# Narrow cross attention: four PSUM banks for scores, one pair for maxima, three key buffers, maxima three steps ahead

## What is computed

```python
def _L1_xattn_ref(queries, keys, values, valid_lens, Wq, Wk, Wv, Wo):
    ...
    q = split_heads(queries @ Wq)
    k = split_heads(keys @ Wk)
    v = split_heads(values @ Wv)
    scores = jnp.einsum('bhqd,bhkd->bhqk', q, k) / jnp.sqrt(jnp.float32(hd))
    mask = jnp.arange(skv)[None, None, None, :] < valid_lens[:, None, None, None]
    scores = jnp.where(mask, scores, NEG)
    p_attn = jax.nn.softmax(scores, axis=-1)
    out = jnp.einsum('bhqk,bhkd->bhqd', p_attn, v)
    out = out.transpose(0, 2, 1, 3).reshape(b, sq, D)
    return out @ Wo
```

## Time and profile before

| what | value |
|---|---|
| median of 3 runs | 4330.43 us (4321.11 to 4331.98) |
| profiled execution, its own time | 4321.63 us |
| its span | 4319.8 us |
| granted TensorE clock, mean | 0.939 |
| TensorE busy | 3752.8 us (87%) |
| VectorE busy | 2665.5 us (62%) |
| ScalarE busy | 2458.7 us (57%) |
| GpSimd busy | 1650.8 us (38%) |

### The profile page before, as it was taken

How to read it: one execution, slowest core, us unless ns; L and a number is a source line. 1 busy time by engine, 2 the same in 40 slices (tenths; PEclk the granted TensorE clock), 3 DMA queues, 4 the chain that set the end, 5 groups by cost and what they waited for, 6 DMA issues and landing times. The chain is left out here.

```text
span 4319.8 us, 77604 instructions
## 1 busy us (share of the span) xinstructions
PE 3752.8 (87%) x28216; PEld 2642.0 (61%) x28216; DVE 2665.5 (62%) x3564; ACT 2458.7 (57%) x4550; POOL 1650.8 (38%) x1365
## 2 busy tenths in 40 slices
PE   5899999999999999999686985788888877667399
PEld 2677777777777777776445984444444443333288
DVE  5766666666666666665174213667767777458577
ACT  2577777777777777676242112466666666535165
POOL 1566666666666666666222002100010000014033
PEclk9999999999999999999787997899999999879699
DMA  5767677776776676663212565776677644100011
GB/s 197 270 247 251 240 260 253 259 249 242 264 251 251 240 248 227 227 222 130 63 23 98 203 244 200 182 155 158 147 156 158 132 71 61 30 19 1 12 50 43
DMA packets 236313, 727.26 MB, mean 168 GB/s; under 512 B 47884, under 2 KB 133132, under 8 KB 167052
## 3 DMA queue, kind: packets, MB, share of 16 engines
q1 hardware_dynamic: 233248, 713.89, 52.8%
q0 software_dynamic: 2688, 8.39, 0.5%
HBM read 627.80 MB, written 94.37 MB: 167 GB/s over the span
## 5 line engine op out<-in xcount | busy, mean ns | idle before, releaser
L752 POOL TENSOR_TENSOR wa_acc<-wa_acc,wa_probs 128x512 f32<-128x512 f32 x960 | 1247.0, 1299 | 524.9 <-ACT wa_probs L613 444.8
L677 DVE TENSOR_REDUCE wa_mx<-wa_ps_m 128x2 f32<-128x1024 f32 x512 | 626.7, 1224 | 486.0 <-PE wa_ps_m L488 485.7
L613 ACT ACTIVATE wa_probs<-wa_ps_s 128x512 f32<-128x512 f32 x1024 | 556.3, 596 | 526.8 <-PE wa_ps_s L534 521.4
L1281 DVE TENSOR_REDUCE na_mx<-na_ps_m 128x2 f32<-128x1024 f32 x512 | 610.5, 1219 | 301.6 <-PE na_ps_m L1105 301.1
L1226 ACT ACTIVATE na_probs<-na_ps_s 128x512 f32<-128x512 f32 x1024 | 556.0, 594 | 406.3 <-PE na_ps_s L1125 406.3
L605 ACT ACTIVATE wa_ps_s<-wa_m_wide 128x512 f32<-128x512 f32 x1024 | 575.7, 605 | 1.0
L510 PE MATMUL wa_ps_o<-wa_probs,wa_values 128*64 128x256 f32 x4096 | 506.5, 390 | 0.0
L449 PE MATMUL wa_ps_k<-wa_k_ctx,wa_w_k 128*128 128x512 f32 x1488 | 389.3, 397 | 0.0
L475 PE MATMUL wa_ps_v<-wa_w_v,wa_v_ctx 128*128 128x256 f32 x2880 | 382.5, 282 | 0.0
L534 PE MATMUL wa_ps_s<-wa_qh,wa_keys 128*128 128x256 f32 x2048 | 381.5, 309 | 0.0
L510 PEld LDWEIGHTS wa_ps_o<-wa_probs,wa_values 128*64 128x64 f32 x4096 | 274.6, 138 | 149.1 <-issue 6.1
(11 more groups left out here) (341 smaller groups left out, 5392.1 us busy)
## 6 DMA issues: line engine op xcount, KB each, us to landing
wa_k_ctx<-ctx_split SPq DMA_DIRECT2D x248, 1024.0 KB, 5.0
wa_v_ctx<-ctx_split SPq DMA_DIRECT2D x120, 1024.0 KB, 5.6
na_ctx<-ctx_split SPq DMA_DIRECT2D x56, 1024.0 KB, 9.0
na_keys<-k_rows SPq DMA_DIRECT2D x384, 128.0 KB
ctx_split<-wa_stage SPq DMA_DIRECT2D x32, 1024.0 KB, 8.8
wa_land<-in_ctxT SPq DMA_DIRECT2D x32, 512.0 KB, 9.6
ge_w_b<-in_w_rows SPq DMA_DIRECT2D x8, 2048.0 KB, 8.4
k_rows<-na_k_high SPq DMA_DIRECT2D x64, 256.0 KB, 4.3
```

The source lines that it names most:

```text
L613: act.activation(probs[:, c % R:c % R + 2, h * SQ:(h + 1) * SQ], ps_s[n % BANKS][:, :].rearrange("p (c n) -> p c n", c=2), ACT.Exp).then_i ...
L677: dve.tensor_reduce(mx[:, half, :, k], ps_m[:, :, :], AX.X, ALU.max).then_inc(m_taken, 1)
L752: pool.tensor_tensor(acc[:, :], acc[:, :], probs[:, c % R, :], ALU.add).then_inc(summed, 1)
L1281: dve.tensor_reduce(mx[:, half, :, k], ps_m[n % 2][:, :, :], AX.X, ALU.max).then_inc(m_taken, 1)
```

## The change

It has four parts, all in `narrow_attention`:

- The eight banks of PSUM are given out anew. Scores get four (`ps_s0` to `ps_s3`, two for even and two for odd steps), and `scores` waits for the exponents of two steps before. The maxima have one pair of banks, `ps_m`, and a unit starts when the unit just before it has been reduced.
- The maxima run three steps ahead (LEAD = 3): in steps 0 to 12 stand units 3 to 15 of pair `a + 1`, in steps 13 to 15 units 0 to 2 of pair `a + 2`. `turn_maximum` and ScalarE's `take_maximum` stand in step 14, and since they use `ps_m`, the unit of step 14 waits for ScalarE's copy.
- There are three buffers of keys. The keys of pair `a + 2` are loaded at the start of pair `a`.
- To make room, `k_low` has the memory of `k_masked` and `w_land` that of `probs`. So masking a block waits until the store of the low part of the block before has landed (`lo_stored`). ScalarE's `take_high` moves from step 14 to 13.

The core of the diff:

```diff
-        k_low = [s.sb(f"k_low{m}", [P, 512], F32R) for m in range(2)]
-        keys = [s.sb(f"keys{i}", [P, SK], F32R) for i in range(2)]
+        k_low = [k_masked[m][:, :].bitcast(F32R) for m in range(2)]
+        keys = [s.sb(f"keys{i}", [P, SK], F32R) for i in range(3)]
...
-        ps_s = [s.ps(f"ps_s{i}", [P, 512]) for i in range(2)]
-        ps_m = [s.ps(f"ps_m{i}", [P, 2, 512]) for i in range(2)]
+        ps_s = [s.ps(f"ps_s{i}", [P, 512]) for i in range(4)]
+        ps_m = s.ps("ps_m", [P, 2, 512])
...
-        def units(t):
-
-            return (0,) if t == 0 else (2 * t - 1, 2 * t) if t < 3 else (t + 2,) if t + 2 < ST else ()
+        LEAD = 3
+
+        def units(a, t):
+
+            if t + LEAD >= ST:
+                taken = [(a + 2, t + LEAD - ST)]
+            elif a == 0 and t < LEAD + 1:
+                taken = [(1, u) for u in ((0,), (1, 2), (3, 4), (5, 6))[t]]
+            else:
+                taken = [(a + 1, t + LEAD)]
+            return [unit for unit in taken if unit[0] < G]
...
-            return ps_m[1][:, 0, :] if half == 0 and n < 4 else ps_p
+            return ps_p if half else ps_s[2]
...
-                if a >= 2:
-                    sp.wait_ge(s_ready, 1 + (a - 2) * CH + (half + 1) * (CH // 2))
+                if a >= 3:
+                    sp.wait_ge(s_ready, 1 + (a - 2) * CH)
...
-                if u == 1:
+                if u == 1 or (a, u) == (1, 0):
                     pe.wait_ge(q_ready, 1 + 2 * a)
-                pe.wait_ge(m_taken, 1 + max(n - 1, 0))
+                pe.wait_ge(m_taken, 1 + n)
...
             def turn_maximum(a):
                 pe.wait_ge(msplit_ready, 1 + a + 1)
+                if 0 < a < G - 1:
+                    pe.wait_ge(m_taken, 1 + (a + 1) * ST + 1)
...
-                pe.wait_ge(exp_done, 1 + n)
+                pe.wait_ge(exp_done, 1 + max(n - 2, 0))
...
                     scores(a, t)
-                    if a + 1 < G:
-                        for u in units(t):
-                            maximum(a + 1, u)
+                    if t == ST - 2 and a + 1 < G:
+                        turn_maximum(a + 1)
+                    if t != ST - 2:
+                        for pair, u in units(a, t):
+                            maximum(pair, u)
...
-                if a + 1 < G:
-                    turn_maximum(a + 1)
+                    if t == ST - 2:
+                        for pair, u in units(a, t):
+                            maximum(pair, u)
...
-                dve.wait_ge(lo_ready, 1 + max(2 * (n - 1) + m + 1, 0))
+                dve.wait_ge(lo_stored[m], 1 + 16 * n)
...
-                    if a + 1 < G:
-                        for u in units(t):
-                            take_maximum(a + 1, u)
+                    if t == 13 and kb is not None:
+                        mask_keys(kb, 1, ps_p)
+                    for pair, u in units(a, t):
+                        take_maximum(pair, u)
+                        if u == ST - 1:
+                            finish_maximum(pair)
...
-                pool.wait_ge(lo_stored[m], 1 + 16 * n)
```

More of the change, by code:

```diff
@@ L921, in narrow_attention @@
         vp_done, v_ready = s.sem("vp_done"), s.sem("v_ready")
-        keys_in = [[s.sem(f"keys_in{i}{half}") for half in range(2)] for i in range(2)]
+        keys_in = [[s.sem(f"keys_in{i}{half}") for half in range(2)] for i in range(3)]
         q_in = [s.sem(f"q_in{i}") for i in range(3)]
@@ L990, in load_keys @@
                     r = h * HEAD
-                    sp.dma_start(keys[a % 2][r:r + KEYS, cols].bitcast(F32), edges[4 * b:4 * b + 4, cols]
-                                 ).then_inc(keys_in[a % 2][half], 16)
+                    sp.dma_start(keys[a % 3][r:r + KEYS, cols].bitcast(F32), edges[4 * b:4 * b + 4, cols]
+                                 ).then_inc(keys_in[a % 3][half], 16)
                     for t in range(3):
                         rows = (2 * b + t % 2) * D + i * W + h * DH
-                        sp.dma_start(keys[a % 2][r + KEYS + t * DH:r + KEYS + (t + 1) * DH, cols].bitcast(F32),
-                                     k_rows[rows:rows + DH, cols]).then_inc(keys_in[a % 2][half], 16)
+                        sp.dma_start(keys[a % 3][r + KEYS + t * DH:r + KEYS + (t + 1) * DH, cols].bitcast(F32),
+                                     k_rows[rows:rows + DH, cols]).then_inc(keys_in[a % 3][half], 16)
             def load_queries(a):
@@ L1056, in _ @@
                     store_keys(k_block(a), 0)
-                if a + 2 < G:
-                    load_keys(a + 2, 0)
-                if k_block(a) is not None:
                     store_keys(k_block(a), 1)
@@ L1124, in scores @@
                         r = slice(h * HEAD, h * HEAD + ROWS)
-                        ins = pe.matmul(ps_s[h][:, i * SQ:(i + 1) * SQ], keys[a % 2][r, (2 * t + i) * P:(2 * t + i + 1) * P],
+                        ins = pe.matmul(ps_s[2 * (t % 2) + h][:, i * SQ:(i + 1) * SQ], keys[a % 3][r, (2 * t + i) * P:(2 * t + i + 1) * P],
                                         q[a % 3][r, :], start=True, stop=True)
@@ L1250, in _ @@
                         take_high(kb, 0)
-                    if t == 14 and kb is not None:
+                    if t == 13 and kb is not None:
                         take_high(kb, 1)
+                    if t == ST - 2 and a + 1 < G:
+                        take_maximum(a + 1)
                     if t == 15 and vb is not None:
                         take_values(vb, 0, ps_p)
-                if a + 1 < G:
-                    take_maximum(a + 1)
         @block.vector
@@ L1341, in _ @@
                         mask_keys(kb, 0, ps_p)
-                    if t == 13 and kb is not None:
-                        mask_keys(kb, 1, ps_p)
-                if a + 1 < G:
-                    finish_maximum(a + 1)
             copy_out(G - 1)
```

24 lines of the change are left out of this document (13 added, 11 removed).

## The result

| what | before | after |
|---|---|---|
| median of 4 runs | 4327.5 us (4321.11 to 4331.98) | 4434.98 us (4426.56 to 4450.84) |
| ratio | 1 | 1.0259, 95% interval 1.0241 to 1.0278 |
| span of the profiled execution | 4319.8 us | 4434.6 us |
| granted TensorE clock, mean | 0.939 | 0.925 |

The forecast was 4374 us with a range of 4335 to 4410. The direction was right; the loss is 107 us where 44 were forecast, and lies outside the range. I read the stretches first, since they answer to the earlier trace rows. The prologue is counted from TensorE's first projection to the first scores (as in the earlier trace rows, where that projection starts at 2646.70), a pair from its first scores to those of the next pair. The windows are the prologue, pair 0, the first 28 us of it, pairs 1 to 20, of these 1 to 5 and 7 to 20, then 21 to 23, 24 to 29, pair 30, and pair 31 up to the end of its division.

The account below looks back on a forecast made before the run. No engine was full; a 1.68 us loop of scores and exponents bound each step, plus pair-end losses. Terms 20 + 8 + 18 − 2 − 1 − 11 + 16 = +48 on 4321.6 gave 4370, as a median 4374; range 4335 to 4410.

Parts of the forecast that it names:

- The loop and its neighbours: Single maxima pair: unit, reduction, next unit every 1.83 us, 29.3 a pair against 26.9, plus VectorE's other work and turning.
- New pairs: Pairs 1 to 20, with keys and values projected: 33.9 us each against 32.9, +20 us for twenty.
- The division: VectorE's dividing takes 2.11 us, outlasts the 0.6 us hand-over and adds 1.4 us a pair.
- masking with turning: Steps 13 to 14 in pairs with projections: masking adds 0.6 us, turning with values projected between adds 2.2.
- the late turning: Step 14 of late pairs: the next unit waits for turning and ScalarE's copies behind its exponents, adding 2.0 us.
- Late: 29.3 + 1.4 + 2.0 = 32.7: Late pairs: loop, division and turning give 32.7 us each against 29.7, +18 us for six.
- Values only: 33.3: Pairs 21 to 23, projecting values but no keys: 33.3 us each against 30.7, +8 us for three.
- The prologue: Mask, copy, GpSimd and store become one loop, 13 us; last units add 3 or 4; +16, bounds 3 to 28.
- Pair 31: Last pair, no maxima beside it: four score banks remove the 1.68 us loop; 21 us, gain 11, bounds 5 to 14.
- Weights did not run ahead: Rival: a waiting unit's weights load early, loop 1.67 us, 77 us less, 4297; chance 0.07.
- Gains at the edges: Rival: cheaper prologue, faster pair 31 and cheaper pair ends cancel the loss, +3, 4329; chance 0.10.
- Keys and stores: Rival: late keys cost TensorE 1 us a pair, late stores make the prologue cost 28, 4416; chance 0.13.

Follow-up runs that it names:

- The two runs that move banks: Changed kernel with two score banks and two maxima pairs as before: 4228.82 us; kernel before with only one maxima pair instead of two: 4575.88 us.
- With 1.3 us less of waiting: Changed kernel with the maxima of pairs 25 to 31 turned in `ps_p`, so step 14's unit need not wait for ScalarE's copy: 4405.5 us, ratio 1.0211.
- another kernel: Changed kernel with two score banks and two maxima pairs as before (4228.82 us); two useless matmuls added in each step of pair 31: 4212.71 us, ratio 0.9758.

## Why the forecast was too low

**The loop and its neighbours: right.** New pairs were forecast at 33.9 us, and pairs 7 to 20, at clock 0.99, are 33.9 but for two of 35.1. A late pair was forecast at 32.7; from 31.2 measured at full clock and 1.3 for the turning I estimate 32.5. The division (1.3 against 1.4), masking with turning (2.8 against 2.8) and the late turning (1.9 against 2.0) each have their row. The two runs that move banks show that taking the second pair from the maxima is the cause: 206 us with the change's order (where scores lose two banks as well), 250 with the old one.

**The step that failed** is the pricing of the late pairs and of pairs 21 to 23: "Late: 29.3 + 1.4 + 2.0 = 32.7" and "Values only: 33.3". I added durations that the earlier trace rows show at clocks of 0.97 and 0.98 and asked only whether TensorE's work fits in at full clock ("TensorE's own work, 1.65 from unit to unit, fits inside"). I did not ask what the new waits do to that clock, although the row of pair 31 beside them had 0.60. At half clock two steps of work are 5.11 us and do not fit into 3.66. Measured were 37.6 for a late pair, 37.7 for pairs 21 to 23, 37.5 for pairs 1 to 5, 31.7 instead of 27.8 for pair 30 and 47.5 instead of 38.9 for pair 0. Against the terms this is 6 × 4.9 + 3 × 4.4 + 22 (pairs 1 to 20) + 4 (pair 30) + 8 (pair 0) = 77 us, less 7 for pair 31, 2 for the prologue and 1 for its earlier start: the 67 that the sum of 48 lacks of 115.

That the low clock causes the length and does not only go with it rests, for the late pairs, on four things. The timeline of pair 24 shows the longer loop at the lower level. Added work made the stretch of pairs 21 to 30 some 25 us shorter, with the clock up from 0.78 to 0.89 in pairs 24 to 29. With 1.3 us less of waiting a pair was 4.4 us shorter (one trace each). And in the last pair of another kernel added work alone gave 9.9 us, with the clock up from 0.59 to 1.00. For pairs 1 to 6 it is only read from the window (0.86), and what starts a fall there stays open.

**The prologue: right number, wrong reason.** +16 was forecast and +14.3 came, but the mask, the copy, "GpSimd's 1.28 and the store are one loop" was to give 13 of it, and it gives nothing: that memory shared alone changes the time by 0.1%. The rest, "3 or 4" for the last units, was too small. One pair alone gave 11 us; six units at the end lie 1.82 to 2.12 us apart, 0.65 to 0.95 more each than in the earlier trace rows, the later ones at the lower clock level, and five blocks before them have two units in a row each. The sentence drawn from the page DMA: Bandwidth & Descriptors of the Trainium skill (section on the anatomy of a DMA) would have made this term nothing, and so it was, though not by its figure: landings here are 3.9 at the median. The page gives that figure for transfers that GpSimd issues and without the time to move the bytes, while these stores are SyncE's, of 256 KB each.

**Pair 31: right mechanism, too timid.** −17.8 against −11. The forecast took 21 us for the steps, between full and half clock, and a tail at half clock "that stays". The clock was 1.00, the exponents ended 17.7 us after the pair's start, and the tail shrank from 6.9 to 4.9. From here on ScalarE ran without a gap, 20 exponents in 10.22 us:

```profile
3874.65 10.22 ACT L1238 ACTIVATE na_probs<-na_ps_s 128x512 f32<-128x512 f32 x20 [0.34 <-PE na_ps_s L1134]
```

Four banks took the wait away, and with it the low clock, which is the same effect that makes the loss elsewhere.

**The rivals.** Weights did not run ahead: units are 1.82 apart and not 1.67. Gains at the edges came (pair 31) and were far too small. Keys and stores were not late: from pair 1 on no engine of the changed kernel waits for a DMA in the view of waits. That rival's 4416 is the nearest number, for a reason that no row shows, so it was near by luck.

## What to carry to other kernels

When banks are moved from one reader to another, work out both loops (hand-over, reading, release) and leave the double buffer with the longer one; a set of banks that is idle in one stretch can be lent there alone, which gave 18 to 19 us here at none of the cost. Then ask of every new wait on TensorE whether its work still fits in at half the granted clock: if it doesn't, price the stretch at both levels and let the range reach to the second.

## What the hardware showed that I had not expected

- Adding useless matmuls made a stretch faster: pairs 21 to 30 went from 371 to 345 us (the kernel from 4434.98 to 4395.89), and the last pair of another kernel from 41.5 to 31.7 us, where the granted clock went from 0.59 to 1.00.
- A loop of 1.83 us with 0.18 us of slack on TensorE (1.65 of work) became one of 2.56 at a granted clock of 0.53 (10.22 us for four).
- Pairs with the same program ran at 33.9 us and clock 0.99, and at 37.5 and 0.86, in one execution (pairs 7 to 20 and 1 to 5). Why the first ones fell and in another kernel did not stays open.
